# Routed experts: activations split in token order and turned by a transposing DMA, with gate and up products two tiles ahead of the down products

## The reference, cut to what matters

```python
gu = jnp.einsum('th,ehf->etf', x, w_gate_up)      # 8 experts, 512 -> 2*256
act = silu(gate) * up
eo = jnp.einsum('eti,eih->eth', act, w_down)      # 256 -> 512
routed = jnp.einsum('te,eth->th', combine, eo)    # combine: top 2 of 8, normalised
```

## Time and profile before

| what | value |
|---|---|
| time, median of 3 runs | 1270.86 us (1269.21 to 1272.81) |
| the profiled execution's own time | 1270.78 us |
| its span in the trace | 1269.0 us |
| PE busy | 1203.0 us (95%) |
| DVE busy | 661.0 us (52%) |
| ACT busy | 476.3 us (38%) |
| POOL busy | 490.1 us (39%) |
| mean granted clock of TensorE | 0.986 of full |

### The profile page before, as it was taken

One profiled execution on the slowest core, in us unless ns is written; L12 is line 12 of the kernel. 1 busy time (PEld: TensorE's weight loads), 2 busy tenths in 40 slices (PEclk: granted clock), 3 DMA queues, 4 the chain that ended last, 5 costly groups with the idle time before them and its releaser, 6 DMA issues. The chain is left out here.

```text
span 1269.0 us, 29255 instructions
## 1 busy us (share of the span) xinstructions
PE 1203.0 (95%) x10768; PEld 815.1 (64%) x10768; DVE 661.0 (52%) x1410; ACT 476.3 (38%) x1030; POOL 490.1 (39%) x432
## 2 busy tenths in 40 slices
PE   4899999999999679999999799999999899999997
PEld 3676777677677357777777344444444477777775
DVE  7888889989998578533333222222222223333333
ACT  6454555555555353322222233333333311111111
POOL 3456656765666200454501122222222044444444
PEclk8999999999999889999999899999999999999999
DMA  6598988788788764334324577887788434444444
GB/s 208 134 254 190 211 234 224 203 224 242 202 218 239 203 202 158 97 105 100 100 100 59 152 184 190 190 198 188 195 193 193 96 133 150 150 149 149 150 150 134
DMA packets 269373, 217.40 MB, mean 171 GB/s; under 512 B 196784, under 2 KB 203056, under 8 KB 269296
## 3 DMA queue, kind: packets, MB, share of 16 engines
q1 hardware_dynamic: 255344, 180.03, 52.9%
q0 software_dynamic: 12848, 35.47, 9.8%
q10 hardware_dynamic: 1104, 0.81, 0.2%
HBM read 115.97 MB, written 56.51 MB: 136 GB/s over the span
## 5 line engine op out<-in xcount | busy, mean ns | idle before, releaser
L570 PE MATMUL sc<-x,WG 128*128 128x256 f16 x3072 | 349.2, 274 | 11.8 <-DVE WD L1780 6.9
L570 PEld LDWEIGHTS sc<-x,WG 128*128 128x128 f16 x3072 | 302.0, 98 | 62.2 <-DVE WD L1780 7.1
L1499 PE MATMUL sc<-WG,raw 128*128 x852 | 209.3, 382 | 6.0 <-DMA raw<-raw 3.7
L1918 DVE SCALAR_TENSOR_TENSOR actv<-sc,up_inv,sg 128x512 f32<-128x512 f32 x64 | 48.0, 750 | 247.2 <-ACT sg L1756 238.0
L1483 POOL DMA_INDIRECT raw<-xs_dram,slots x71 | 67.3, 948 | 281.5 <-DMA raw<-raw 209.3
L1756 ACT ACTIVATE sg<-sc,gate_inv 128x512 f32<-128x512 f32 x64 | 44.0, 687 | 308.8 <-PE sc L570 249.2
L1506 PE MATMUL yp<-WD,ah 128*128 128x512 f16 x512 | 152.3, 379 | 0.7 <-DVE al L1923 0.7
L1499 PEld LDWEIGHTS sc<-WG,raw 128*128 128x128 f16 x852 | 83.9, 98 | 92.4 <-issue 9.1
L1986 POOL DMA_INDIRECT raw<-y_dram,gidx x64 | 64.2, 1004 | 151.8 <-DVE ys L1899 102.3
L839 PE MATMUL ring<-WG 128*128 128x256 f16 x1024 | 119.6, 273 | 2.4 <-PEq L241 2.0
L2123 DVE TENSOR_TENSOR alr<-rat,ahr 128x256 f16<-128x256 f32 x71 | 30.1, 424 | 158.6 <-ACT ahr L2100 151.0
(11 more groups left out here) (260 smaller groups left out, 1778.3 us busy)
## 6 DMA issues: line engine op xcount, KB each, us to landing
y_dram<-raw SPq DMA_DIRECT2D x71, 256.0 KB
WG<-in_L_attn_x SPq DMA_DIRECT2D x32, 512.0 KB, 5.3
WG<-in_L_ffn_w_gate_up SPq DMA_DIRECT2D x16, 512.0 KB, 4.7
xs_dram<-WG SPq DMA_DIRECT2D x16, 512.0 KB, 3.7
xT_dram<-x SPq DMA_DIRECT2D x16, 512.0 KB, 2.7
x_dram<-x SPq DMA_DIRECT2D x32, 256.0 KB, 2.1
x<-xT_dram SPq DMA_DIRECT2D x16, 512.0 KB
x1s<-x_dram SPq DMA_DIRECT2D x16, 512.0 KB
```

Source lines behind the costliest of these rows:

```text
L570: ins = pe.matmul(gu[:, h, f * 2 * P:(f + 1) * 2 * P].rearrange("p (u t) -> p u t", u=2), w[:, kk, b, part * P:(part + 1) * P], x[:, :, a ...
L1499: ins = pe.matmul(gu[bank], x(kk, a), w[:, 0, kk, b, :], start=(i == 0), stop=(i == len(done) - 1))
L1918: v.scalar_tensor_tensor(out=actv[:, g % 2], in0=gu[g % 2][:, 1].rearrange("p (f t) -> p f t", f=FT), scalar=up_inv[:, 1:2], in1=sg[:], op ...
```

## The change

The transposes on TensorE go. VectorE's product `actv` is split in token order into `act_hl` (high part by ScalarE, low part by VectorE, both now from SBUF), and SyncE turns both parts with one transposing DMA of 128 rows by 512 float16 into `act_T` (`turn_act`), again two buffers. TensorE makes the products of tile r+2 in one piece and then the down product of tile r. SyncE's order becomes: turn of tile r+4, turn_act of tile r, store of tile r-1. ScalarE's step becomes Silu(r), high part(r), y_evac(r-2). A turn_act waits for the low part of its tile and for the down product of two tiles before. The PSUM tensors `at` are no longer used.

```diff
-                ah = sb(c, "ahr", [P, 2, FT, P], F16)
-                al = sb(c, "alr", [P, 2, FT, P], F16)
+                act_hl = sb(c, "act_hl", [P, 2, 2, FFN], F16)
+                act_T = sb(c, "act_T", [P, 2, 2, FT, P], F16)
...
-                    turn(sp, 2, S["sp_passed"])
+                    def turn_act(r):
+                        wait_apart(sp, S["al_ready"], r + 1, S["sp_passed"])
+                        if r > 1:
+                            wait_apart(sp, S["y_full"], r - 1, S["sp_passed"])
+                        sp.dma_start_transpose(act_T[:, r % 2].rearrange("p s f t -> p (s f) t"),
+                                               act_hl[:, r % 2].rearrange("p s c -> p (s c)")).then_inc(act_turned[r % 2], 16)
+
+                    for r in (2, 3):
+                        turn(sp, r, S["sp_passed"])
                     for r in range(SLOT_TILES):
-                        if r + 3 < SLOT_TILES:
-                            if r + 3 >= XH:
-                                wait_apart(sp, S["gu_full"], r + 3 - XH + 1, S["sp_passed"])
-                            turn(sp, r + 3, S["sp_passed"])
-                        store(r)
+                        if r + XH < SLOT_TILES:
+                            wait_apart(sp, S["gu_full"], r + 1, S["sp_passed"])
+                            turn(sp, r + XH, S["sp_passed"])
+                        turn_act(r)
+                        if r > 0:
+                            store(r - 1)
+                    store(SLOT_TILES - 1)
...
-                    def tile(r, own, nxt):
-
-
-                        par, last = r % 2, r == SLOT_TILES - 1
-                        if not last:
-                            pe.wait_ge(turned[(r + 1) % XH], 16 * ((r + 1) // XH + 1))
-                            if r > 0:
-                                pe.wait_ge(S["act_ready"], r)
-                            gate_up_rows(pe, gu, 1 - par, slot_rows(r + 1), WG[:, nxt], FIRST)
-                        pe.wait_ge(S["act_ready"], r + 1)
-                        for f in range(FT):
-                            ins = pe.transpose(at[par][:, f, :], actv[:, par, f * P:(f + 1) * P], ident[:])
-                        ins.then_inc(S["at_full"], 1)
-                        if not last:
-                            gate_up_rows(pe, gu, 1 - par, slot_rows(r + 1), WG[:, nxt], REST).then_inc(S["gu_full"], 1)
-                        else:
+                    def products(r, e):
+                        pe.wait_ge(turned[r % XH], 16 * (r // XH + 1))
+                        if r > 1:
+                            pe.wait_ge(S["act_ready"], r - 1)
+                        gate_up_rows(pe, gu, r % 2, slot_rows(r), WG[:, e], range(3 * KT)).then_inc(S["gu_full"], 1)
+
+                    def tile(r, own, ahead):
+
+
+                        par = r % 2
+                        if r + 2 < SLOT_TILES:
+                            products(r + 2, ahead)
+                        elif r == SLOT_TILES - 1:
+                            pe.wait_ge(S["act_ready"], SLOT_TILES)
                             pe.wait_ge(x_ins[1][0], 16)
                             gate_up(pe, gu_whole[0], xT[:, 0], WG[:, 0]).then_inc(gu_fulls[1], 1)
...
-                        pe.wait_ge(S["al_ready"], r + 1)
-                        down(pe, yp[par], (ah[:, par], al[:, par]), WD[:, own], True, True).then_inc(S["y_full"], 1)
+                        pe.wait_ge(act_turned[par], 16 * (r // 2 + 1))
+                        down(pe, yp[par], (act_T[:, par, 0], act_T[:, par, 1]), WD[:, own], True, True
+                             ).then_inc(S["y_full"], 1)
...
+                        act.wait_ge(S["act_ready"], r + 1)
                         if not first:
-                            y_evac(*((q, 0) if par == 1 else (q - 1, 1)))
-                        act.wait_ge(S["at_full"], r + 1)
-                        act.activation(ah[:, par], at[par][:], ACT.Copy).then_inc(S["ah_ready"], 1)
+                            act.wait_ge(act_turned[par], 16 * q)
+                        act.activation(act_hl[:, par, 0], actv[:, par], ACT.Copy).then_inc(S["ah_ready"], 1)
+                        if not first:
+                            y_evac(q - 1, par)
...
-                        v.tensor_tensor(al[:, par], at[par][:], ah[:, par], ALU.subtract).then_inc(S["al_ready"], 1)
+                        v.tensor_tensor(act_hl[:, par, 1], actv[:, par], act_hl[:, par, 0], ALU.subtract
+                                        ).then_inc(S["al_ready"], 1)
```

More of the change, by code:

```diff
@@ L2004, in routed @@
                 actv = sb(c, "actvr", [P, 2, FFN])
-                ah = sb(c, "ahr", [P, 2, FT, P], F16)
-                al = sb(c, "alr", [P, 2, FT, P], F16)
+                act_hl = sb(c, "act_hl", [P, 2, 2, FFN], F16)
+                act_T = sb(c, "act_T", [P, 2, 2, FT, P], F16)
                 ysb = raw[:, 1, 0:2]
                 gu = gu_half
-                at = [c.enter_context(nc.psum_tensor(f"rat{i}", [P, FT, P], F32)) for i in range(2)]
                 yp = [c.enter_context(nc.psum_tensor(f"ryp{i}", [P, DIM], F32)) for i in range(2)]
-                names = ("act_ready sg_ready at_full ah_ready al_ready y_full y_ready cw_ready sp_passed")
+                names = "act_ready sg_ready ah_ready al_ready y_full y_ready cw_ready sp_passed"
                 S = {x: sem(c, "r_" + x) for x in names.split()}
@@ L2014, in routed @@
                 y_out = [sem(c, f"ry_out{i}") for i in range(2)]
+                act_turned = [sem(c, f"act_turned{i}") for i in range(2)]
                 block = c.enter_context(nc.Block())
@@ L2019, in run_steps @@
                     step(0, 0, True)
-                    step(0, 1, False)
+                    step(0, 1, True)
                     with eng.Fori(1, SLOT_TILES // 2) as q:
@@ L2071, in tile @@
+                    def tile(r, own, ahead):
[4 more added lines that the diff above has]
+                            pe.wait_ge(S["act_ready"], SLOT_TILES)
                             pe.wait_ge(x_ins[1][0], 16)
                             gate_up(pe, gu_whole[0], xT[:, 0], WG[:, 0]).then_inc(gu_fulls[1], 1)
-                        after = expert_of(pe, r + 2) if r + 2 < SLOT_TILES else None
+                        after = expert_of(pe, r + 3) if r + 3 < SLOT_TILES else None
@@ L2074, in tile @@
                         if r > 1:
                             pe.wait_ge(S["y_ready"], r - 1)
-                        pe.wait_ge(S["al_ready"], r + 1)
-                        down(pe, yp[par], (ah[:, par], al[:, par]), WD[:, own], True, True).then_inc(S["y_full"], 1)
-                        return after
-                    own, nxt = expert_of(pe, 0), expert_of(pe, 1)
+                        pe.wait_ge(act_turned[par], 16 * (r // 2 + 1))
+                        down(pe, yp[par], (act_T[:, par, 0], act_T[:, par, 1]), WD[:, own], True, True
+                             ).then_inc(S["y_full"], 1)
@@ L2081, in _ @@
+                        return after
+                    places = [expert_of(pe, r) for r in range(3)]
+                    products(1, places[1])
                     for r in range(SLOT_TILES):
-                        own, nxt = nxt, tile(r, own, nxt)
+                        places = places[1:] + [tile(r, places[0], places[2])]
                 @block.scalar
@@ L2096, in step @@
                                        ).then_inc(S["sg_ready"], 1)
+                        act.wait_ge(S["act_ready"], r + 1)
                         if not first:
-                            y_evac(*((q, 0) if par == 1 else (q - 1, 1)))
-                        act.wait_ge(S["at_full"], r + 1)
-                        act.activation(ah[:, par], at[par][:], ACT.Copy).then_inc(S["ah_ready"], 1)
+                            act.wait_ge(act_turned[par], 16 * q)
+                        act.activation(act_hl[:, par, 0], actv[:, par], ACT.Copy).then_inc(S["ah_ready"], 1)
+                        if not first:
+                            y_evac(q - 1, par)
                     run_steps(act, step)
+                    y_evac(SLOT_TILES // 2 - 1, 1)
                     y_evac(SLOT_TILES // 2, 0)
```

## The result

The changed kernel takes 1292.88 us (median of 4 runs, 1288.88 to 1295.04) against 1271.55 us: a ratio of 1.0155, with a 95% interval of 1.0121 to 1.0189. It is 1.6% slower. The forecast was 1267 us, in a range of 1256 to 1290.

A forecast was written before the change was run, and what follows sets the result against it. The prediction took TensorE to bound the routed stage, with the DMA engines next. From 1270.78 us it took 5.2 us gained over 68 tiles and added 1.6 us for start and end: 1267.2 us, range 1256 to 1290.

The forecast's parts named there:

- TensorE's floor: Routed stage: if nothing else delayed TensorE, a tile would take 3.885 us and 68 tiles would gain 15.0 us.
- the part removed: Two transposes per tile on TensorE, said to cost 0.22 us each tile on the path.
- The splits: High and low parts on ScalarE and VectorE, costed at nothing beside TensorE's work; at most 0.8 us per tile uncovered.
- The ring: Down product through y_evac, store, turns on SyncE to the down product two tiles later: at least 4.48 us plus landing.
- X = 3.5: Time in us from the act turn's issue to its landing, giving a tile of 4.03 us.
- the crowded value: Landing of the act turn if delayed like the median turn: 3.65 us.
- the quiet one: Landing of the act turn alone: 2.45 us.
- the point of 3.73: Landing in us at which a tile costs as much as before, 4.106 us; slower from there on.
- Start and end: Both ends of the routed stage: 1.3 us lost at the start and 0.3 at the end, 1.6 us in sum.
- The load: DMA work per tile goes from 3.33 to 4.03 us, the added turn taking 0.70; a share of 1.04.
- the rival of a full DMA system: DMA work of 4.03 us per tile sets the pace, nothing measurable, 1267 to 1272 us; chance 0.08.
- the longer ring: Rival: act turn lands after 4.3 us or more, tile 4.39 us, kernel 1292 us; chance 0.30.

The follow-up runs named there:

- deeper: Changed kernel with products three tiles ahead, the store three behind, four buffers each for products, act_T and act_hl: 1257.98 us, 0.9868 of the kernel before.
- store_late: Changed kernel with SyncE storing tile r-2 in place of tile r-1 behind turn_act(r): 1272.16 us, ratio 0.9988 to the kernel before.
- more_turns: Kernel before the change plus one transposing DMA of 128 x 512 float16 per tile that nobody reads: 1278.45 us, ratio 1.0045.
- no_gather: Changed kernel without the gathers of tiles 4 to 70: 1263.34 us (one run).
- rolled_late: Changed kernel with TensorE's tiles 4 to 67 in a hardware loop of four and the store one tile later: 1271.09 us, ratio 0.9990.
- pool_code: Changed kernel without those gathers, plus 50 semaphore increments per tile on GpSimd: 1262.02 us (one run).
- rolled: Changed kernel with TensorE's tiles 4 to 67 in a hardware loop of four tiles: 1306.22 us, ratio 1.0260 to the kernel before.
- more_code: Changed kernel plus 40 semaphore increments per tile on TensorE's sequencer: 1591.33 us (one run).

## Why the prediction was wrong, step by step

- *TensorE's floor and the part removed: right.* 0.22 us per tile, 15 us in all. deeper collects it.
- *The splits cost nothing: right.* From SBUF they take 416 and 425 ns, against 384 and 424, beside TensorE's work.
- *The ring: the right mechanism.* It was found in the right place, its fixed part was 4.30 us in the median and 4.44 in the mean where 4.28 was forecast, and store_late, which breaks it, takes away the whole loss of 21 us.
- *Its last term, X = 3.5: this step failed.* The prediction put one number for the landing, "nearer the crowded value than the quiet one". The median is 3.8 and the mean 3.92, both over the point of 3.73 from which the same text had the change slower, and the landings spread to 5.7. Over tiles 8 to 63, where TensorE stood over 0.1 us ahead of a down product (33 of 56), the act turn was issued 4.39 us behind the down product of two tiles before, and the next down product started 4.59 us later: 8.98 us for two tiles. The forecast had 8.06. All 56 tiles took 4.49 us in the mean, all 68 took 4.43, in place of 4.03, and 68 x 0.40 = 27 us, less the 1.6 us for start and end that did not come, is the error of 26 us.
- *How much of that is size and how much spread.* With the measured means, two tiles take 4.44 + 3.92 + 0.27 = 8.63 us, 4.31 each: the larger part of the way from 4.03. The rest is spread. The rival gave this its name: a stall of TensorE is never made up, so slow landings count in full and quick ones give nothing. An estimate from the trace bears it out: taking tile for tile the later of TensorE's own 3.885 us and the ring, with each tile's issue and landing (drawn from the 28 recorded ones where one is missing), gives 4.44 us in place of 4.31. In such a ring a term that varies can't stand for its mean.
- *Start and end: 1.6 us forecast, about nothing measured.* From the start of tile 0's products to the last down product, the stage is 21.5 us longer, and the ring accounts for that. Why the start cost nothing can be read in part: the products of tile 2 took 4.1 us (719.70 to 723.79), where before they and two transposes took 5.4 (718.93 to 724.33), at a granted clock of 0.72 from 720 to 725 us in place of 0.58. The forecast had reckoned with the lower clock.
- *The load: half seen.* The share went from 0.81 to 0.95, and is 1.09 in deeper, which hardly stalls; 1.04 was forecast. Per tile that is 0.95 x 4.43 = 4.2 us of the 16 engines in place of 4.03: the added turn took 0.9 us, not 0.70 (collisions are in this number). That the load costs 6 us even where nobody waits for the new turn (more_turns) was not in the sum: the rival of a full DMA system had it as no change.
- *The rival that came true* was the longer ring, forecast at 1292 us with X at 4.3, and given 3 in 10. Its time was right in part by luck: X did not reach 4.3 but stayed at 3.8 in the median (4.2 in the mean where TensorE waited), a longer fixed part and the spread made up for it, and the 1.6 us for start and end that it also added did not come.
- *The range did not fit the chances.* The longer ring had a chance of 0.30 and a time of 1292 us, and the range ended at 1290, with 2 in 10 left for all that lies outside. By its own numbers the text should have gone past 1292.

What stays open: how much of the spread is due to the 16 KB instruction fetches. In no_gather each late landing had one in flight, but in rolled_late turns land as late without any, and no run took the fetches away and left all else alone.

## What to carry to other kernels

When an operation moves from a busy engine to a DMA, draw the ring that its result closes, every instruction of the issuing queue included, and ask what is left if the landing is the slowest seen, not the median (here 5.7 against 3.8 us). If the ring is near the time that the bound engine needs, break it before anything else: one store moved a tile later was worth 21 us here, and a tile more of distance, with four buffers in place of two for the products, act_T and act_hl, turned 1.6% slower into 1.3% faster. A full DMA system (a share of 1.09 in deeper) cost 1.0 us of 248 once the landings had a tile more in hand.

## What the runs showed of the hardware

- A transposing DMA of 128 x 512 float16 occupies SyncE's queue for 1.19 us and one of 128 x 1024 for 1.30 us: the issue hardly goes with size. The landing does: 2.5 us in the median without gathers (no_gather), against 3.2 for a large turn alone.
- With one gather per tile beside it, the small turn landed 1.3 us later in the median (3.8 against 2.5 us).
- An act turn with a 16 KB instruction fetch in flight had its last packet 1.1 us later than one without, with and without gathers. With an 8 KB fetch alone it landed 0.3 us later in the mean (pool_code: 2.8 against 2.5 us).
- With a hardware loop on TensorE and its register loads, TensorE stood for some 2.5 to 3.8 us at each turn-over in rolled. In rolled_late most of them took less than 1.3 us; why is not shown.
- 40 increments of a semaphore held TensorE up for 3.6 us per tile (more_code), although nothing waited for them.
